# Second attention: ScalarE evicts one bank of transposed probabilities in every second step

## The reference, cut to what matters

```python
x = x + _L1_xattn_ref(_layernorm(x), ctx_1024, ctx_1024, ...)
# inside:
scores = jnp.einsum('bhqd,bhkd->bhqk', q, k) * scale
probs = jax.nn.softmax(scores, axis=-1)
out = jnp.einsum('bhqk,bhkd->bhqd', probs, v)
out = out.transpose(0, 2, 1, 3).reshape(B, S, EMB)
return out @ Wo.T + bo
```

## Time and profile before

| what | value |
|---|---|
| median of 3 runs | 1800.08 us (1799.65 to 1801.08) |
| the profiled execution's own time | 1800.79 us |
| its span, first to last instruction | 1799.1 us |
| TensorE busy over the span | 85% |
| VectorE, ScalarE, GpSimd busy | 61%, 50%, 23% |
| second attention, stretch of the trace | 1141 to 1374 us |

### The profile page before, as it was taken

How to read it: one execution, slowest core, us unless ns; L and a number is a source line. 1 busy time by engine, 2 the same in 40 slices (tenths; PEclk the granted TensorE clock), 3 DMA queues, 4 the chain that set the end, 5 groups by cost and what they waited for, 6 DMA issues and landing times. The chain is left out here.

```text
span 1799.1 us, 28913 instructions
## 1 busy us (share of the span) xinstructions
PE 1531.8 (85%) x9520; PEld 1191.5 (66%) x9520; DVE 1094.3 (61%) x2186; ACT 894.0 (50%) x2217; POOL 407.5 (23%) x377
## 2 busy tenths in 40 slices
PE   4899999999999999609999592799996469999967
PEld 3678777777777787605666482565654358888857
DVE  6877777777778767522333246577776644444447
ACT  2776767676767777211111221565653144444432
POOL 6110101000010100230000304332310134444425
PEclk9999999999999999659999795899997589999988
DMA  3300000000000000039986200000000023333324
GB/s 114 105 3 13 1 13 2 13 2 13 2 13 1 1 1 1 1 109 340 317 316 225 88 1 29 24 7 13 7 1 1 1 86 102 108 119 101 106 56 117
DMA packets 66459, 115.78 MB, mean 64 GB/s; under 512 B 6208, under 2 KB 46144, under 8 KB 66336
## 3 DMA queue, kind: packets, MB, share of 16 engines
q1 hardware_dynamic: 61392, 99.66, 17.0%
q0 software_dynamic: 4944, 14.55, 2.3%
HBM read 97.68 MB, written 16.52 MB: 63 GB/s over the span
## 5 line engine op out<-in xcount | busy, mean ns | idle before, releaser
L435 ACT ACTIVATE a_p<-a_s,a_negmax 128x512 f32<-128x512 f32 x256 | 176.2, 688 | 157.1 <-DVE a_negmax L603 115.4
L603 DVE TENSOR_REDUCE a_negmax<-a_s 128x1 f32<-128x512 f32 x256 | 176.1, 688 | 49.1 <-PE a_s L298 39.1
L207 POOL TENSOR_TENSOR a_o_l<-a_o,a_o_h 128x256 fp32r<-128x256 f32 x64 | 47.1, 735 | 560.5 <-ACT a_o_h L460 560.5
L1517 ACT ACTIVATE h_probs<-h_scores,h_negmax 128x256 f32<-128x256 f32 x256 | 118.0, 474 | 83.1 <-DVE h_negmax L1684 83.1
L307 PE MATMUL a_t<-ident,a_p 128*128 128x128 f32 x1024 | 157.0, 276 | 0.7 <-DVE a_pT L618 0.7
L307 PEld LDWEIGHTS a_t<-ident,a_p 128*128 128x128 f32 x1024 | 120.8, 140 | 53.1 <-issue 18.3
L2091 POOL TENSOR_TENSOR n_w_l<-n_raw,n_w_h 128x768 fp32r<-128x768 f32 x64 | 118.3, 1849 | 147.5 <-ACT n_w_h L2061 147.5
L597 DVE TENSOR_TENSOR a_k_hl<-a_k_p,a_k_hl 64x512 fp32r<-64x512 f32 x128 | 88.1, 688 | 70.9 <-ACT a_k_hl L418 69.8
L325 PE MATMUL a_out_p<-a_pT,a_v 128*64 128x256 f32 x1024 | 124.6, 385 | 0.0
L297 PE MATMUL a_s<-a_k_hl,a_q_hh 128*128 128x512 f32 x256 | 108.5, 424 | 8.7 <-ACT a_p L435 6.8
L2165 DVE TENSOR_TENSOR n_hidden<-n_up,n_silu 128x512 f32<-128x512 f32 x64 | 44.3, 692 | 115.8 <-PE n_up L2113 113.1
(11 more groups left out here) (347 smaller groups left out, 4374.9 us busy)
## 6 DMA issues: line engine op xcount, KB each, us to landing
e_w_in<-in_L_ffn_gate_up_proj SPq DMA_DIRECT2D x31, 1024.0 KB, 6.4
n_raw<-in_L_ffn_w SPq DMA_DIRECT2D x64, 384.0 KB, 3.0
e_w_out<-in_L_ffn_down_proj SPq DMA_DIRECT2D x31, 512.0 KB, 4.4
chosen_out<-n_result POOLq DMA_DIRECT2D x16, 256.0 KB, 4.5
u_y<-chosen_out SPq DMA_DIRECT2D x8, 512.0 KB, 4.0
rows_in<-a_zeros SPq DMA_DIRECT2D x1, 3968.0 KB, 15.5
e_rows<-rows_in SPq DMA_DIRECT2D x31, 128.0 KB, 4.2
rows_out<-e_result POOLq DMA_DIRECT2D x31, 128.0 KB, 4.1
```

The lines of the kernel that those rows point to most:

```text
L435: act.activation(probs[j][:, :], scores[j % 2][:, :], ACT.Exp, bias=negmax[:, j:j + 1], accum_out=total[:, r % 2, j % 2, j // 2:j // 2 + 1 ...
L603: dve.tensor_reduce(negmax[:, j:j + 1], scores[j % 2][:, :], AX.X, ALU.max, negate=True).then_inc(max_set, 1)
L1517: ins = act.activation(probs[s % 4][:, j, :], scores[s % 2][:, j // 2, j % 2, :], ACT.Exp, bias=negmax[:, s % 4, j:j + 1], accum_out=total ...
```

## The change

In odd steps the second bank of transposed probabilities is copied by ScalarE (an activation with Copy) and no longer by VectorE. ScalarE does it after the exponentials of two steps later: exponent(3), then the copy for step 1; exponent(5), then that of step 3; exponent(7), then that of step 5; exponent(1) of the next batch, then that of step 7. Where `high_o`, `set_k` or `set_q` follow in the same step, they come after the copy. The semaphores and their values stay as they are.

```diff
+                def set_turned(b, s):
+                    n = STEPS * b + s
+
+                    wait(act, o_done, n // 4 - 1)
+                    h = s // 2 % 2 * FOUR + 2
+                    act.wait_ge(turned[1], n + 1)
+                    act.activation(probsT[s // 4][:, h:h + 2, :, P:2 * P], turned_p[1][:, :, :, :], ACT.Copy).then_inc(evened[1], 1)
...
                 for b in range(NB):
                     for s in range(STEPS):
                         exponent(b, s)
+                        if s % 2 and s > 2:
+                            set_turned(b, s - 2)
+                        elif s == 1 and b:
+                            set_turned(b - 1, STEPS - 1)
                         if s == 3 and b:
                             high_o(b - 1, 1)
...
+                set_turned(NB - 1, STEPS - 1)
                 high_o(NB - 1, 1)
...
                     wait(dve, o_done, n // 4 - 1)
-                    for i in range(2):
+
+                    for i in range(2 - s % 2):
                         h = s // 2 % 2 * FOUR + 2 * i
                         dve.wait_ge(turned[i], n + 1)
                         dve.tensor_copy(probsT[s // 4][:, h:h + 2, :, s % 2 * P:(s % 2 + 1) * P],
```

## The result

The changed kernel takes 1803.71 us, median of 20 runs (1796.97 to 1810.97); the kernel before takes 1799.24 in 20 runs beside it (1797.36 to 1803.13). The ratio is 1.0026, with a 95% interval of 1.0016 to 1.0036: 4.5 us slower. I had forecast 1799.9 and a range up to 1803.4. The scatter is a finding of its own: the standard deviation of a run is 1.5 us before and 3.4 us after.

The account below looks back on a forecast made before the run. TensorE was taken to set the pace. Six boundaries gain 2.4 us, batch 0 loses 1.2 and batch 7 1.0: -0.2 us, so 1800.6 for the profiled execution, 1799.9 as median, range 1797.2 to 1803.4.

Parts of the forecast that it names:

- the clock: Rival: holes in batches 0 and 7 each cause a slow-clock stretch, up to 1.75 us each, 1801.7 or 1803.4; chance 0.10.
- The sign that I had set for it: The prediction is wrong if the clock of the second attention's stretch falls below 0.99.
- What bounds the stage: Second attention: TensorE, busy 157.2 of 166 us, sets the pace; 13.0 us of its waits are for VectorE's copies.
- VectorE's relief: Batch boundary: VectorE runs 0.60 us earlier, so turn(7) no longer waits; net 0.40 us gained at each of six boundaries.
- The second half of turn(6): Batch boundary: waits for ScalarE's copy and starts at 1252.44 instead of 1251.94, 0.50 us lost.
- The three margins of 0.13, 0.14 and -0.06 us: Middle batches: time to spare for ScalarE's copies before turn(2), turn(0) and turn(4); the last is late but costs nothing.
- the margins are gone: Rival: ScalarE frees the bank later than summed; 0.2 us later costs 3.5 us, giving 1803.4; chance 0.14 of passing 3.6.
- Batch 0: No output projection covers turn(4), which waits for ScalarE's copy: 1.18 us lost.
- Batch 7: No projections cover turn(0) and turn(2), which wait for ScalarE's copies: +1.0 us together, boundary 6 to 7 included.
- First in, first out on ScalarE: Skill's rule: the bank lies full until the exponentials ahead of its copy finish; by that alone some 6 us slower.
- only the relief counts: Rival: ScalarE's copies come as early as VectorE's did; 4.5 us gained over seven boundaries, 1795.6; chance 0.08.
- the tail's +0.2: Last batch's turn(6) loses up to 0.5 us, partly hidden at 1.2 GHz; counted as +0.2 us.

Follow-up runs that it names:

- experiment 6: Kernel before, plus five filler transposes of the identity into an idle tile ahead of every turn(6) and turn(7): 1800.60 us against 1799.90, ratio 1.0000.
- experiment 5: Changed kernel with filler transposes into an idle tile in its holes (batch 0, every turn(6), batch 7): 1799.65 us against 1799.90, ratio 0.9996.
- experiment 7: Changed kernel, with a spare 128x512 addition on VectorE in place of each copy it had given up: 1809.13 us, ratio 1.0042.
- experiment 1: Changed kernel with nine filler transposes between the two halves of turn(4) of batch 0: 1800.46 us against 1799.42, ratio 1.0012.
- experiment 3: Changed kernel with ScalarE's same 32 copies behind the first of the four exponentials instead of the fourth: 1795.80 us, ratio 0.9974.
- experiments 2 and 10: Changed kernel, ScalarE copying only from step 5 of batch 0 to step 5 of batch 6, VectorE elsewhere: 1800.07 us, then 1795.40 (ratios 1.0001, 0.9982).
- experiment 4: The changed kernel measured again without an edit: 1802.63 us, ratio 1.0017.

## Why the prediction was wrong

The forecast, 1799.9, failed in one step: the clock. The sum has no term for it, and as a rival it got a chance of 0.10, on the argument that two idles of 0.7 and 0.8 us at each boundary had left the clock at 1.00. That argument holds for the kernel before (experiment 6), but not for holes of another size and place. The changed kernel's clock fell three times in its first trace (10.2 us in all) and twice in the second before the tail (10.2 us again), at 1.6 us per 3.4 us: 4.8 to 4.9 us, where the sum had nothing. The price itself was right, up to 1.75 us a stretch by the earlier trace rows; I had allowed for one or two stretches in batches 0 and 7, and none at a middle boundary. The sign that I had set for it came: over the stage the clock was 0.98. With the holes filled no fall was left before 1360 us and the loss was gone (experiment 5). The rule of the Trainium skill (TensorE: Matmul & The Clock Gate, What's actually happening), that the low rate is the default which activity lifts, stood beside this rival. The runs agree with it as far as falls came behind holes and filling the holes removed them; that a hole of 1.78 us left the clock at full once shows how little it says of the single hole.

The other steps, point by point:
- What bounds the stage, and where VectorE's relief enters: right. A middle batch lost 0.44 us where 0.40 was forecast. Experiment 7 shows the relief as its cause.
- The second half of turn(6): forecast 0.50 late. Its start lies 0.97 behind the first half instead of 0.51, so 0.46.
- The three margins of 0.13, 0.14 and -0.06 us held in every middle batch, with a copy of 0.608 us where I had 0.588. The rival "the margins are gone" was named with a price near the measured time (1803.4 from its point on) but is not what happened.
- Batch 0: 1.18 us forecast for the hole, 1.17 measured in experiment 1 (21.63 against 20.46).
- Batch 7: 0.8 of the 1.0 us up to its last score; 26.23 us in experiment 5, where no fall lies in it, against 25.45 in experiment 6, 0.78. The tail took 14.7 us instead of 15.3; its own fall of the clock was absent in this trace.
- First in, first out on ScalarE: the copy's place in the queue decides. Moved from behind the fourth exponential to behind the first, the same copies make the kernel 0.26% faster than before instead of 0.26% slower (experiment 3). The prediction gave the rival "only the relief counts" 0.08, because the copy sits behind the exponentials. So it does in this change; what I didn't ask is which other place in the queue it could have.

In the trace the sum closes. Holes and relief: 1.17 in batch 0, 6 x -0.44 = -2.6, 0.78 in batch 7, together -0.7 us (-0.2 was forecast, with the tail's +0.2 in it). Three falls: 4.9. Tail: -0.7. That is 3.5 of the 3.6 us.

Open: what decides behind which hole and in which execution the clock falls, and why the kernel of experiments 2 and 10 gave 1800.1 once and 1795.4 once, beyond that its runs had a lower clock the first time. Each trace is one execution, so how many falls the median run has was not counted. That the falls make up the 4.5 us of the median rests on experiment 5, run on another chip, and on the recorded clock of the runs.

## What to carry to other kernels

Where TensorE sets the pace, read a change's waits twice: once for their length and once as holes in TensorE's work, since 3.4 us at half clock cost more than a hole of half or one microsecond does. An eviction handed to another engine's in-order queue is worth what its place there is worth; ask first when the bank fills and put the copy right there, not at the end of the group. And when runs of a changed kernel scatter twice as wide as before, look at the granted clock before looking for a dear instruction. Fillers are a tool for finding this out more than a remedy: where no fall was, they gained nothing.

## What the runs showed of the hardware

- The clock fell to 1.2 GHz for 3.4 or 6.8 us in a stage in which TensorE is busy for 216.8 of 232 us. In the changed kernel it fell right after a hole of 1.05 us (at 1158.6) and one of 1.03 us (at 1346.4), and once after holes of 0.72 and 0.35 us within 1.7 us (at 1226.9). Such a pair stands at seven boundaries of an execution; in the two executions of this kernel three of the fourteen were followed by a fall. The same hole of batch 0 in another execution left it at 1.00 (experiment 4), and so did one of 1.78 us in the tail of the changed kernel's first trace (1364 to 1376).
- At half clock the changed kernel's batches took 1.6 us longer for every 3.4 us of it (28.25 against 29.87 and 31.40).
- With work of no use in the holes that exist anyway no fall was seen behind them: nine filler transposes, 1.15 us, in batch 0's (experiments 1 and 5, one trace each).
- ScalarE's copy of 128x512 took 0.608 us here and 0.588 in the first attention, the same form and shape. Behind the first exponential it took 0.59.
